# A two-layer graph network on one NeuronCore: where in a step the first layer's sums, roots and early sums stand, and how far behind its units run

## What is computed

```python
# first layer
msg_input = concatenate([h[src], h[dst], edge_feat], axis=-1)
messages = silu(msg_input @ W1 + b1) @ W2 + b2
agg = segment_sum(messages, dst)
h_new = silu(concatenate([h, agg], axis=-1) @ W3 + b3) @ W4 + b4
x1 = layernorm(x + (h_new + x))
# second layer, h = x1
agg = segment_sum(h[src], dst)
z = (1.0 + eps) * h + agg
z = relu(z @ W1 + b1) @ W2 + b2
ln = layernorm(z + h) * gamma + beta
out = layernorm(x1 + relu(ln))
```

## Time and profile before

| what | value |
|---|---|
| time, median of 3 runs | 1918.95 us (1912.32 to 1919.72) |
| the profiled execution's own time | 1915.15 us |
| its span | 1913.0 us |
| mean granted TensorE clock | 0.874 |
| PE / DVE / ACT / POOL busy | 76% / 53% / 33% / 58% |
| gathers of the first layer (L869) | 784, from the start to about 1,280 us |

### The profile page before, as it was taken

How to read it: one execution, slowest core, us unless ns; L and a number is a source line. 1 busy time by engine, 2 the same in 40 slices (tenths; PEclk the granted TensorE clock), 3 DMA queues, 4 the chain that set the end, 5 groups by cost and what they waited for, 6 DMA issues and landing times.

```text
span 1913.0 us, 31192 instructions
## 1 busy us (share of the span) xinstructions
PE 1449.5 (76%) x8093; PEld 1148.8 (60%) x8093; DVE 1016.9 (53%) x2306; ACT 631.5 (33%) x1257; POOL 1102.2 (58%) x1164
## 2 busy tenths in 40 slices
PE   5357777777777778777777777886488888888893
PEld 5245555555555556566565565664377777777773
DVE  5137775565654444445444454444245656766666
ACT  4223444444444444444444444342001111111110
POOL 2656666666666666565565555662366666666640
PEclk8677888888888899899899888888699999999996
DMA  5222232232335334343333333322466666656631
GB/s 187 73 53 73 77 79 76 78 81 74 80 83 96 93 97 106 100 101 99 100 98 101 98 97 102 100 71 77 138 190 184 177 181 184 186 176 190 186 104 30
DMA packets 189123, 214.13 MB, mean 112 GB/s; under 512 B 60426, under 2 KB 149517, under 8 KB 189011
## 3 DMA queue, kind: packets, MB, share of 16 engines
q1 hardware_dynamic: 138399, 131.62, 23.0%
q0 software_dynamic: 36352, 74.52, 16.3%
q10 hardware_dynamic: 14260, 6.68, 1.2%
HBM read 202.74 MB, written 9.85 MB: 111 GB/s over the span
## 4 chain that ended last, share of the span: by engine, by line
PE 31%; another core or an unknown queue 29%; issue 19%; ACT 10%; DVE 5%; ACTq 3%; DVEq 1%; SPq 1%; DMA 1%; POOLq 0%; POOL 0%
PE bank L1404 5%; PE bank L1206 5%; PE bank L1210 4%; PE bank L1380 4%; PE bank L1220 4%; ACT msg L1014 2%; PE bank L1353 2%; ACTq L994 2%; PE bank L1332 2%; ACT L1027 1%; PE bank L1366 1%; ACT terms_r L1006 1%; ACT terms_l L1005 1%; ACT S L1068 1%
## 5 line engine op out<-in xcount | busy, mean ns | idle before, releaser
L869 POOL DMA_INDIRECT gath<-src_term,src_col x784 | 752.1, 959 | 479.8 <-issue 211.0
L869 POOL DMA_INDIRECT gath<-layer_input,src_col x336 | 326.2, 971 | 210.8 <-PE bank L1332 105.0
L1206 PEld LDWEIGHTS bank<-terms_r,terms_l 128*128 128x128 f32 x1568 | 250.4, 228 | 193.5 <-issue 191.4
L1206 PE MATMUL bank<-terms_r,terms_l 128*128 128x128 f32 x1568 | 270.0, 316 | 119.6 <-issue 112.1
L1220 PE MATMUL bank<-oh,msg 128*128 128x128 f32 x1568 | 227.8, 293 | 100.8 <-issue 84.0
L1220 PEld LDWEIGHTS bank<-oh,msg 128*128 128x128 f32 x1568 | 212.6, 206 | 145.5 <-issue 118.7
L1210 PE MATMUL bank<-gath,ident 128*128 128x512 f32 x392 | 242.9, 701 | 19.6 <-issue 19.4
L1896 DVE TENSOR_TENSOR S<-S,bank 128x128 f32 x98 | 28.2, 288 | 416.6 <-remote 279.6
L1885 DVE TENSOR_SCALAR_CACHE_REDUCE terms_l<-dst_bc,node_col 64x512 f32<-64x512 int32 x196 | 222.0, 1133 | 41.4 <-issue 35.5
L1404 PE MATMUL bank<-S 128*128 128x288 f32 x672 | 193.9, 443 | 37.3 <-ACT S L1068 28.3
L1404 PEld LDWEIGHTS bank<-S 128*128 128x128 f32 x672 | 136.9, 209 | 86.7 <-issue 47.5
(11 more groups left out here) (208 smaller groups left out, 1768.9 us busy)
## 6 DMA issues: line engine op xcount, KB each, us to landing
dst_bc<-in_dst SPq DMA_DIRECT2D x195, 128.0 KB
xT<-sorted_src SPq DMA_DIRECT2D x42, 512.0 KB
xs<-layer_input SPq DMA_DIRECT2D x136, 128.0 KB
gath<-src_term,src_col POOLq DMA_INDIRECT x784
terms_l<-layer_input SPq DMA_DIRECT2D x88, 128.0 KB
terms_r<-layer_input SPq DMA_DIRECT2D x88, 128.0 KB
msg<-layer_input SPq DMA_DIRECT2D x80, 128.0 KB
ef_s<-in_edge_attr SPq DMA_DIRECT2D x97, 64.0 KB
```

The lines of the kernel that those rows point to most:

```text
L869: g.indirect_dma_start(out=gath[:, slot, j * D:(j + 1) * D], out_offset=None, in_=table[0:rows, :], in_offset=bass.IndirectOffsetOnAxis(ap ...
L1206: mm(bank[h][:, j * D:(j + 1) * D], terms_l[:, u, h, j, :], terms_r[:, u, h, j, :], start=j == 0, stop=False)
```

## The change

Five things are moved; no operation is added or dropped, but for one wait each.

1. DVE adds a pair's sums at the front of the step after the one in which it did so far (`add_sums`, lag 3 to 4), ahead of that step's windows, one-hots and sort work.
2. Every stage of a unit runs two steps later, on all engines and for SP's loads too. PE: `hidden0` 7 to 9, `out0` 8 to 10, `turn_x1` 10 to 12. ACT: `hidden0` 8 to 10, `store0` 10 to 12, `start_T` 11 to 13, `std0` 9 to 11. DVE: `rows0` and `norm0` 9 to 11. POOL: the root 9 to 11. SP: 9 to 11.
3. ACT does the root ahead of the messages, not behind them.
4. PE does the early sums ahead of the early rows of its step.
5. `out0` uses the free upper half of bank 3 and no longer bank 2, so the wait `hnew_read` is gone. The sort's transposes take the other one of banks 2 and 3, with a wait on the sums of five steps before in place of four, and one wait for one-hots (`oh_made`) is new in step 44.

```diff
             return [of_unit_in(0, FIRST_BEFORE, lag, lambda j: body(j, bank[6])),
-                    of_unit_in(FIRST_BEFORE, UNITS - 1, lag, lambda j: body(j, bank[2])),
+                    of_unit_in(FIRST_BEFORE, UNITS - 1, lag, lambda j: body(j, bank[3][:, XW:2 * XW])),
                     of_unit_in(UNITS - 1, UNITS, lag, lambda j: body(j, bank[0]))]
...
         FIRST_EARLY = SORTED + 2
-        FIRST_BEFORE = (FIRST_EARLY + 3 - 8) // 2
+        FIRST_BEFORE = (FIRST_EARLY + 3 - 10) // 2
         TURNS = (21, 22, 24, 25, 28, 29, 31, 32, 35, 36, 40, 41)
...
             sp.wait_ge(consts, 1)
-            steps(sp, NPAIR - 2, (1, SORTED, SORTED + 1, SORTED + 2), of_unit(9, load_unit0), of_pair(0, load_pair),
+            steps(sp, NPAIR - 2, (1, SORTED, SORTED + 1, SORTED + 2), of_unit(11, load_unit0), of_pair(0, load_pair),
                   at_steps({1: load_weights, SORTED: store_chunks, SORTED + 1: load_bases,
...
             pool.wait_ge(src_ready, 1)
-            skewed(NPAIR + BRIDGED, [(0, gather_sources), (9, rsqrt0_of)])
+            skewed(NPAIR + BRIDGED, [(0, gather_sources), (11, rsqrt0_of)])
             either_order(pool, ordered1, any_order)
...
             steps(act, NPAIR - 2, range(STEPS), at_steps({s: lambda s=s: zero_part(s) for s in range(STEPS)}),
-                  of_unit(8, hidden0), of_unit(10, store0), of_unit(11, start_T),
-                  of_pair(1, edge_features), of_pair(0, window_x), of_pair(2, messages(0)),
-                  of_early(2, keep_early), of_pair(2, messages(1)),
-                  of_unit(9, lambda j: None if rsqrt_on_pool(j) else std0(j)))
+                  of_unit(10, hidden0), of_unit(12, store0), of_unit(13, start_T),
+                  of_pair(1, edge_features), of_pair(0, window_x),
+                  of_unit(11, lambda j: None if rsqrt_on_pool(j) else std0(j)),
+                  of_pair(2, messages(0)), of_early(2, keep_early), of_pair(2, messages(1)))
             either_order(act, ordered1, any_order)
...
                 pe.wait_ge(misfits_made, 6)
-                pe.wait_ge(sums_added, done(SORTED - 4))
-                mm(bank[2 + SORTED % 2][0:1, XW:XW + 6], ones[:, 0:1], misfits[:, :],
+                pe.wait_ge(sums_added, done(SORTED - 5))
+                mm(bank[3 - SORTED % 2][0:1, XW:XW + 6], ones[:, 0:1], misfits[:, :],
                    start=True, stop=True).then_inc(misfits_summed, 1)
...
 
-                pe.wait_ge(sums_added, done(s - 4))
-                return bank[2 + s % 2]
+                pe.wait_ge(sums_added, done(s - 5))
+                return bank[3 - s % 2]
 
...
 
-            def hnew_read(j):
-
-                pe.wait_ge(v_made, done(j))
-
             def early_rows(e, m, q):
...
             steps(pe, NPAIR - 2, (4,) + TURNS + tuple(s + 1 for s in TURNS) + (SORTED, SORTED + 1),
-                  of_early(3, early_kept), of_pair(1, turn_ef), of_pair(2, pre_sums), of_early(2, early_rows),
-                  of_early(3, early_sums), (0, NPAIR, keys_taken),
-                  of_unit_in(FIRST_BEFORE, UNITS - 1, 9, hnew_read), of_pair(3, message_sums),
+                  of_early(3, early_kept), of_pair(1, turn_ef), of_pair(2, pre_sums), of_early(3, early_sums),
+                  of_early(2, early_rows), (0, NPAIR, keys_taken), of_pair(3, message_sums),
                   at_steps({4: weight_products}),
-                  of_unit(10, ordered_turn_x1), *in_banks(8, ordered_out0), of_unit(7, ordered_hidden0),
+                  of_unit(12, ordered_turn_x1), *in_banks(10, ordered_out0), of_unit(9, ordered_hidden0),
                   (0, NPAIR, turn_keys))
...
                 elif s == SORTED + 1:
+                    dve.wait_ge(oh_made, done(SORTED - 1))
                     ve_.tensor_copy(iota1_ps, iota_w[:, :]).then_inc(iota1_kept, 1)
...
 
-            steps(dve, NPAIR - 2, range(1, SORTED + 2), at_steps({5: weight_products}), *in_banks(9, rows0),
-                  of_early(4, add_early), of_pair(1, windows), of_pair(2, one_hots(0, sums_ps, oh_made)),
-                  of_unit(9, ordered_norm0), of_pair(3, add_sums), (0, NPAIR, sort_edges),
-                  of_early(1, early_hots))
+            steps(dve, NPAIR - 2, range(1, SORTED + 2), at_steps({5: weight_products}), *in_banks(11, rows0),
+                  of_early(4, add_early), of_pair(4, add_sums), of_pair(1, windows),
+                  of_pair(2, one_hots(0, sums_ps, oh_made)),
+                  of_unit(11, ordered_norm0), (0, NPAIR, sort_edges), of_early(1, early_hots))
             either_order(dve, ordered1, any_order)
```

More of the change, by code:

```diff
@@ L1743, in take_rows @@
                 dve.wait_ge(keys_turned, n)
-                ve_.tensor_scalar(key_rows[:, h * XW:(h + 1) * XW], bank[2 + s % 2][0:ROWS, XW:2 * XW],
+                ve_.tensor_scalar(key_rows[:, h * XW:(h + 1) * XW], bank[3 - s % 2][0:ROWS, XW:2 * XW],
                                   sign[:, b:b + 1], None, ALU.mult).then_inc(keys_read, 1)
@@ L1770, in take_chunks @@
                 dve.wait_ge(keys_turned, n)
-                ve_.tensor_copy(src_chunks[:, h * XW:(h + 1) * XW], bank[2 + s % 2][:, XW:2 * XW]) \
+                ve_.tensor_copy(src_chunks[:, h * XW:(h + 1) * XW], bank[3 - s % 2][:, XW:2 * XW]) \
                     .then_inc(keys_read, 1)
@@ L1796, in count_misfits @@
                 dve.wait_ge(misfits_summed, 1)
-                ve_.tensor_reduce(misfit_sum[:, :], bank[2 + SORTED % 2][0:1, XW:XW + 6], AX_X, ALU.add) \
+                ve_.tensor_reduce(misfit_sum[:, :], bank[3 - SORTED % 2][0:1, XW:XW + 6], AX_X, ALU.add) \
                     .then_inc(misfits_added, 1)
```

2 lines of the change are left out of this document (1 added, 1 removed).

## The result

| | before | changed |
|---|---|---|
| median of 20 runs each | 1914.21 us | 1923.62 us |
| range | 1907.33 to 1922.76 | 1912.03 to 1930.46 |
| ratio | | 1.0043, 95% interval 1.0028 to 1.0058 |
| profiled execution, its span | 1915.15, 1913.0 us | 1930.46, 1928.3 us |

The change makes the kernel slower by 0.43%, 8 us (the medians lie 9.4 us apart), where 19 us of gain were forecast. The median lies inside the range of 1864 to 1935 us that was given, but on the slower side of the kernel before. The profiled execution of the changed kernel is the slowest of its 20, so that the spans differ by 15.3 us and not by 8 to 9.

The account below looks back on a forecast made before the run. A circle of waits bounds the kernel, PE's order deciding from 640 us on, above POOL's floor. Terms -20 + 0 + 0 - 2.3 + 3 = -19.3 us, from the 1918.95 us median, gave 1900 us; range 1864 to 1935 us.

Parts of the forecast that it names:

- DVE's long wait: DVE, 640 to 1250 us: 270 us idle ahead of the add of a pair's sums, called mostly a symptom.
- The floor of some 12 us a pair: POOL's gathers, 130 to 640 us: a pair takes 12.2 us at most, which nothing on DVE or ACT shortens.
- The swap, -20 us: PE from 640 us on: early sums ahead of early rows fill the wait for ACT, at most 24.5 us gained.
- Rival A: PE is behind its records, so filling gaps gains nothing: 1920 us, chance 0.25.
- The prediction's own test: Changed profile: idle time ahead of early rows near zero, POOL's mean wait 2.7 to 2.8 us; wait not shorter means Rival A.
- The root, 0 us: ACT: root and table loads ahead of messages, 2.85 us in odd steps, hidden; 16 us cost if POOL's cover goes.
- rival C: 130 to 640 us: late messages in odd steps cost 16 us, early sums gain nothing: 1939 us, chance 0.18.
- The 14 us of table loads: ACT: 11 loads of 1.28 us leave its chain, not added, being the same wait that the early sums fill.
- The adds, 0 us: DVE: sums added at the front of the next step; what queues behind them is hidden, 0 us.
- The start, -2.3 us: DVE at the start: gives the turned weight back to PE at about 120.8 us instead of 123.14.
- The units later, +3 us: End of the first layer: last units finish later behind the last pair's sums, +3 us, bounds 2 and 7.
- Rival B: From 640 us on: PE's idle spots go, the granted clock rises, 54 us won: 1866 us, chance 0.17.

Follow-up runs that it names:

- f3: Kernel before with only DVE's adds of the sums moved to the front of the next step: 0.9994 of before (1942.5 us).
- g4: Kernel before with only two of a pair's eight message products, part of the messages left out of the sums: 0.9740 of before (1913.9 us).
- g3: Kernel before with only the swap, early sums ahead of early rows on PE: 1.0121 of before (1913.9 us).
- g1: Changed kernel with the swap undone, early rows ahead of early sums again: 0.9987 of before (1913.9 us).
- f4: Kernel before with only ACT's root moved ahead of the messages: 0.9973 of before (1942.5 us).
- f2: Kernel before with only the units run two steps later: 1.0062 of before (1942.5 us).
- g2: Changed kernel with ACT's root put back behind the messages: 1.0083 of before (1913.9 us).
- f1: The changed kernel itself, run once more: 1.0097 of before (1942.5 us).
- h3: Kernel before with the swap, and PE's turn of edge features moved behind the pair's products: 1.0028 of before (1517.5 us).
- h4: Kernel before with only PE's turn of edge features moved behind the pair's products: 1.0643 of before (1517.5 us).
- e3: Kernel before with only the swap, early sums ahead of early rows on PE: 0.9997 of before (1517.6 us).

## Why the prediction was wrong, and where it was right

**What bounds the kernel.** That PE's order decides the stretch from 640 us on was right for the chips of 1914 and 1943 us, and DVE's long wait was a symptom, as argued: with the adds moved it fell from 270 to 97 us, and alone (f3) that was worth nothing. The floor of some 12 us a pair held in every version on the chip of 1914 us but g4 (pairs 16 to 52 in 429 to 432 us), but it is no floor of POOL's own: on the chips of 1518 us the same pairs take 363 to 365 us.

**The swap, -20 us: the failing step.** This is the first term of the sum. The gap ahead of the early rows went, 32.1 to 7.4 us. But the prediction took the rows' later end for free, with the sentence that PE wants the kept rows "only in its next step, some 12 us on". PE wants them at the very front of that step, ahead of everything (`early_kept`), because turned edge features and early rows share bank 4. In the step that the prediction read, the rows end at 853.81 us and PE's next turn stands at 857.19 (PE's timeline, kernel before):

```profile
857.19 0.27 PE L1193 MATMUL bank<-ident,ef_s 128*128 128x128 f32 x1
```

That is 3.4 us of cover by the records, not 12. Of this the swap takes the 1.1 us of the early sums, while on these chips the release of the rows can come 8 us after their recorded end, and came later than those 3.4 us in 30 of 45 steps of g3, for 3 of 46 before. Measured: +23 us alone (g3), and 1.0043 to 0.9987 when undone (g1), about 11 us.

**Rival A** had the cause in its hand, an add that starts 4.8 us after the record says that PE was done, and drew only half of it: if PE is behind its records, filling gaps gains nothing. The other half is that every wait on PE's products then has less cover than the records show. It was argued against with the 0.04 us between the rows' end and ACT's copy, a step in which PE had just waited; three other steps of the same trace show 4.3 to 4.6 us in its place. The Trainium skill ("Perfetto Trace Analysis", per-instruction lifecycle) calls TensorE's recorded end an estimate; the traces of this case agree, with 8.16 us between record and copy in g3 (761.51 to 769.67). The prediction's own test read the trace rightly: gap gone, POOL's wait not shorter (3.79 us, not 2.7 to 2.8), so not the forecast but A. That A's time, 1920 us, is near the measured 1923.6 is luck: A puts the swap at nothing, and it costs some 11 us here, while the root, which A leaves out, gives some 5 back.

**The root, 0 us,** bounds to +16: it came out at -5 us (f4, 0.9973), and rival C, which put 16 us on late messages from 130 to 640 us, did not happen. Pairs 16 to 52 took 431.3 us before and 429.3 us after. The 14 us of table loads that would leave ACT's chain were not added to the sum; whether f4's 5 us are a part of them isn't shown.

**The adds, 0 us:** right (0.9994). **The start, -2.3 us:** not shown. In the result's two profiles the turned weight came back at 119.34 us for 123.14 and POOL's pair 7 starts 4.4 us earlier. But in other kernels with the adds at their old place it came back at 122.94 (g3), 115.89 (f4), 113.12 (f2) and 111.57 us (g4), in those with the adds in front at 119.40 to 120.11 us (g1, g2, f1, f3). The spread between single executions is wider than the term.

**The units later, +3 us,** bounds 2 and 7. In the profile the tail behind the last pair's sums grew from 16.1 us (1306.08 to 1322.15) to 19.1 us (1318.55 to 1337.66). On the chips of 1518 us the runs give some 3.5 us. On the chip of 1943 us f2 gave 12 us, 8 to 17, which is over the upper bound. Its trace, of the fastest of its runs, has a tail 5.4 us longer than f3's and 8.6 us longer than f4's, and pairs 52 to 92 in 543.7 us, 2 us more than theirs; the rest has no place found. DVE's largest new wait, for SP's load of x, which stands behind SP's wait for the early rows, comes with the adds (f3) and not with the units (f2). The adds' term missed it, and it cost nothing that was measured.

**Rival B** came out the other way: PE's idle time was moved, not removed, and the granted clock fell from 0.91 to 0.87. What it expected of the clock did show in h3 beside h4, where idle time of PE did go, and the granted clock rose from 0.92 to 1.00.

In sum: +3 (tail), -5 (root, from the chip of 1943 us) and 0 (adds) give -2 us, as g1 has it (0.9987), and the swap's +11 us in their company makes +9 us of it, beside the measured 8 to 9. The granted clock is in each of these differences and has no term of its own. The lower bound of the forecast's terms, 1896 us, is 1894 us when added up (1919 - 24.5 - 2.3 + 2), which changes nothing. No version beats the kernel before on both kinds of chip. The root alone wins 0.27% on one and was not run on the other; with the adds it costs 0.11 to 0.15% there. The changed kernel without the swap is at 0.9987 and 1.0026.

## What to carry to other kernels

A gap filled by moving work ahead of an instruction makes that instruction's result later: ask who reads it, and what the same engine needs back from that reader at the front of its next step, above all through a shared PSUM bank. In this case a matmul's recorded end held where PE had just waited for someone; where it ran on without a wait, look at when the waiting engine really starts, and take the cover as shorter by that. And a hidden wait may guard an engine's pace by being in the cheap place: removing it can move it to a dear one.

## What the runs showed of the hardware

The same kernel took 1914, 1943 or 1518 us, and the runs taken together on one chip stayed with one of these within 1%. The granted clock, 0.87 against 0.95, is one difference. Another is who is named for a wait: on a chip of 1518 us the profile puts POOL's and ACT's waits down to PE's instructions, promptly after their recorded end, and PE waits for the gathered rows; on the others most of these waits before 640 us, and most of ACT's after, are "remote" and end later than any record of PE explains. Waits of PE in e3 (1518 us), 200 to 600 us:

```profile
PE bank L1210 <- DMA gath<-src_term,src_col: 81.5, 42, 10.3
...
ACT msg L1014 <- PE bank L1210: 83.0, 32, 12.2
```

and of ACT in the kernel before (1914 us), same stretch:

```profile
ACT terms_l L1005 <- remote: 105.0, 27, 6.7
```

What makes PE's releases late there was not found.
